# Turning attention probabilities: TensorE and ScalarE's share given to VectorE and to transfers

## What is computed

```python
x = x + tanh(g_ffn[0]) * ffn(layernorm(x))
# ffn, per sample: T = 512 positions, 8 heads of 64, 5 experts of which each head takes 2
q, k = heads(x @ Wq), heads(x @ Wk)
v = einsum('bthe,btek->bhtk', top2(x @ Ws) * sigmoid(x @ Ws), x @ Wv)
probs = softmax(q * 64 ** -0.5 @ k.T)      # 512 x 512 for each head
attn = probs @ v
out = einsum('bthe,bthk,ekd->btd', top2_mask(x @ Wd), attn, Wo)
```

## Time and profile before

| | before |
|---|---|
| times of three executions | 1172.51, 1174.29, 1174.52 us |
| median | 1174.29 us |
| the profiled execution's own time | 1175.16 us |
| its span | 1173.4 us |
| TensorE busy | 1128.9 us, 96% |
| VectorE busy | 915.4 us, 78% |
| ScalarE busy | 634.2 us, 54% |
| GpSimd busy | 657.0 us, 56% |
| share of TensorE in the chain that ended last | 71% |
| transfers | 108.44 MB, 30.7% of the 16 DMA engines' time |

### The profile page before, as it was taken

How to read it: one execution, slowest core, us unless ns; L and a number is a source line. 1 busy time by engine, 2 the same in 40 slices (tenths; PEclk the granted TensorE clock), 3 DMA queues, 4 the chain that set the end, 5 groups by cost and what they waited for, 6 DMA issues and landing times.

```text
span 1173.4 us, 19136 instructions
## 1 busy us (share of the span) xinstructions
PE 1128.9 (96%) x5885; PEld 855.5 (73%) x5885; DVE 915.4 (78%) x1656; ACT 634.2 (54%) x1332; POOL 657.0 (56%) x476
## 2 busy tenths in 40 slices
PE   7999999999999999999999999999999999999998
PEld 6788888888888888876767667667666666667655
DVE  7988887878787857476786886887887886976986
ACT  7634343434343433457566556556556565666654
POOL 2635242424242425439389298397497496595693
PEclk9999999999999999999999999999999999999999
DMA  5341414141414123422323324224233233231140
GB/s 199 143 135 45 135 46 133 46 132 47 132 49 130 57 86 115 148 89 72 90 55 109 88 54 138 59 63 151 54 89 107 54 110 104 52 122 48 47 126 37
DMA packets 76606, 108.44 MB, mean 92 GB/s; under 512 B 7712, under 2 KB 40224, under 8 KB 76576
## 3 DMA queue, kind: packets, MB, share of 16 engines
q1 hardware_dynamic: 76576, 108.07, 30.7%
HBM read 58.76 MB, written 16.78 MB: 64 GB/s over the span
## 4 chain that ended last, share of the span: by engine, by line
PE 71%; DVE 11%; ACT 7%; issue 7%; POOL 3%; DMA 1%; DVEq 0%; ACTq 0%
PE ps_f L992 22%; PE ps_o L2267 9%; PE ps_s L992 7%; PE ps_h L992 6%; PE ps_r L2193 6%; PE ps_r L2226 4%; PE ps_s L2244 4%; ACT probs_odd L1663 4%; PE ps_r L2202 3%; DVE nmax L1853 3%; PE ps_s L2252 3%; DVE z_tmp L1872 2%; ACT tmp L1663 1%; POOL spare L1580 1%; DVE z L1883 1%
## 5 line engine op out<-in xcount | busy, mean ns | idle before, releaser
L1853 DVE TENSOR_REDUCE nmax<-ps_s 128x1 f32<-128x512 f32 x256 | 158.4, 679 | 75.0 <-PE ps_s L2244 74.0
L1580 POOL TENSOR_TENSOR spare<-xv,pick 128x512 f32<-128x512 f32 x160 | 170.6, 1066 | 35.8 <-DVE pick L1968 22.9
L1598 POOL TENSOR_TENSOR z<-z,z_tmp 128x1280 f32<-128x1280 f32 x35 | 102.8, 2937 | 156.0 <-DVE z_tmp L1872 153.7
L1586 POOL TENSOR_TENSOR spare<-spare 128x512 f32<-128x512 f32 x128 | 180.5, 1410 | 10.0
L1663 ACT ACTIVATE probs_odd<-ps_s,nmax 128x512 f32<-128x512 f32 x124 | 146.7, 1183 | 0.0
L1663 ACT ACTIVATE tmp<-ps_s,nmax 128x512 f32<-128x512 f32 x124 | 85.6, 690 | 102.6 <-DVE nmax L1853 102.6
L2267 PE MATMUL ps_o<-pt,spare 128*64 128x512 f32 x496 | 115.0, 606 | 2.3 <-issue 2.3
L254 POOL TENSOR_TENSOR e_t<-e_t 128x512 fp32r<-128x512 f32 x28 | 35.4, 1302 | 135.8 <-ACT e_t L510 135.8
L2244 PE MATMUL ps_s<-k,q 64*128 64x512 f32 x768 | 106.5, 408 | 0.9 <-ACT pt L1672 0.9
L2244 PEld LDWEIGHTS ps_s<-k,q 64*128 64x128 f32 x768 | 67.4, 184 | 46.9 <-issue 34.3
L2252 PE MATMUL ps_s<-ident,probs_odd 128*128 128x128 f32 x512 | 77.4, 279 | 19.6 <-ACT probs_odd L1663 17.9
(11 more groups left out here) (245 smaller groups left out, 2302.0 us busy)
## 6 DMA issues: line engine op xcount, KB each, us to landing
pt<-tmp SPq DMA_DIRECT2D x248, 128.0 KB, 2.6
stage<-in_x SPq DMA_DIRECT2D x32, 256.0 KB, 3.1
x_sb<-in_x SPq DMA_DIRECT2D x8, 1024.0 KB, 5.3
x_dram<-x_sb SPq DMA_DIRECT2D x32, 256.0 KB, 3.2
stage<-x_dram SPq DMA_DIRECT2D x8, 1024.0 KB, 5.5
x_sb<-x_dram SPq DMA_DIRECT2D x8, 1024.0 KB, 5.5
out_dram<-x_sb SPq DMA_DIRECT2D x31, 256.0 KB, 2.6
stage<-in_ctx_t SPq DMA_DIRECT2D x28, 256.0 KB, 2.8
```

The lines of the kernel that those rows point to most:

```text
L1580: pool.tensor_tensor(v_tmp[:] if e else acc, xv[:, :, e, :].unsqueeze(2).broadcast_to(shape), pick[:, e, :, 2 * p:2 * p + 2].unsqueeze(3). ...
L1586: pool.tensor_tensor(acc, acc, v_tmp[:], ALU.add).then_inc(v_steps, 1)
L1598: pool.tensor_tensor(zv, zv, z_tmp[:, h % 2], ALU.add).then_inc(z_pool, 1)
L1853: dve.tensor_reduce(nmax[:, n:n + 1], ps_s[:, n % BANKS, :], AX_X, ALU.max, negate=True).then_inc(nmax_ready, 1)
```

## The change

All four steps of a round go the way of the even ones. Both halves of a round's buffer hold two heads, so `tmp` has room for one round only, and a second buffer, `late`, is laid behind `spare`, which for that is allocated as a part of a larger tile. The order of a buffer's columns gets the head as a further factor, so that a block row's run is 2 KB long, and each of the four transfers of a round carries 256 KB; `pt` has the two heads of a pair interleaved likewise. VectorE turns four tiles in TURNS, TensorE none; `probs_copy`, `probs_odd` and the waits for them are gone, and TensorE writes a bank of `ps_s` again when its exponential is done. ScalarE waits once a round for the move of the round before the last. In the last two rounds of the last sample TensorE turns as before; there ScalarE writes the exponentials in the order of the output and reads the scores with a stride.

```diff
-        probs_even = both.tmp[:].rearrange("p r (j s a) -> p (r j s a)", s=2, a=BLOCK).rearrange(
-            "p (r j s a) -> p r j s a", r=2, s=2, a=BLOCK)
-        probs_odd = sb("probs_odd", [P, BANKS // 2, T])
+        probs = both.tmp[:].rearrange("p k t -> p (k t)"), both.late
...
-        def even_probs(n):
-            return probs_even[:, n // BANKS % 2, :, n % BANKS // 2, :]
+        def blocks(n):
+
+            return probs[n // BANKS % 2].rearrange("p (j i s a) -> p j i s a", i=2, s=2, a=BLOCK)[:, :, n % 2,
+                                                                                              n % BANKS // 2, :]
...
+        def by_rows(p):
+
+            return pt[:, p % 2 * 2:p % 2 * 2 + 2].rearrange("p i k t -> p (i k t)").rearrange(
+                "p (r q k i s a) -> p r q k i s a", r=2, q=QUADS, k=NT, i=2, s=2)
...
             def move_blocks(b, r, first=False):
 
                 p = r // 2
-                sp.wait_ge(blocks_turned, b * ODD_STEPS + (r + 1) * ODD_ROUND)
+                sp.wait_ge(blocks_turned, b * STEPS + (r + 1) * BANKS)
...
                 for q in range(QUADS):
-                    sp.dma_start(by_rows(2 * p % 4)[:, r % 2, q].rearrange("p k s a -> p (k s a)"),
-                                 probs_even[q * BLOCK:(q + 1) * BLOCK, r % 2].rearrange(
-                                     "p (j k) s a -> p j (k s a)", j=QUADS)).then_inc(moved[r % 2], 16)
+                    sp.dma_start(by_rows(p)[:, r % 2, q].rearrange("p k i s a -> p (k i s a)"),
+                                 probs[r % 2][q * BLOCK:(q + 1) * BLOCK].rearrange(
+                                     "p (j u) -> p j u", j=QUADS)).then_inc(moved[r % 2], 16)
...
             def scores_exp(b, n, first):
                 act.wait_ge(nmax_ready, b * STEPS + n + 1)
                 h, t = head_tile(n)
-                scores = ps_s[:, n % BANKS, :]
-                if n % 2 == 0:
-                    if n >= 2 * BANKS or not first:
-
-                        act.wait_ge(moved[n // BANKS % 2], (b * PAIRS + n // PAIR) * MOVED)
-                    out, scores = even_probs(n), scores.rearrange("p (j a) -> p j a", a=BLOCK)
-                else:
-                    if n >= BANKS or not first:
-
-                        act.wait_ge(pt_ps, odd_turned(b, n - BANKS))
-                    out, scores = by_keys(probs_odd[:, n % BANKS // 2, :]), by_scores(scores)
...
+                if n % BANKS == 0 and (n >= 2 * BANKS or not first):
+
+                    act.wait_ge(moved[n // BANKS % 2], (b * PAIRS + n // PAIR) * MOVED)
+                act.activation(blocks(n), ps_s[:, n % BANKS, :].rearrange("p (j a) -> p j a", a=BLOCK), ACT.Exp,
+                               bias=nmax[:, n:n + 1], accum_out=den[:, h, t:t + 1]).then_inc(p_exp, 1)
...
-                act.activation(by_keys(plain_probs(n)), by_scores(ps_s[:, n % BANKS, :]), ACT.Exp, bias=nmax[:, n:n + 1],
+                act.activation(plainly(plain_probs(n)), scores_by_keys(ps_s[:, n % BANKS, :]), ACT.Exp, bias=nmax[:, n:n + 1],
...
-                    if 0 <= n < ROUNDS:
-                        for tile in range(n * BANKS + 1, n * BANKS + BANKS, 2):
-                            probs_copy(b, tile, first)
...
-                dve.transpose(even_probs(n), even_probs(n)).then_inc(blocks_turned, 1)
+                dve.transpose(blocks(n), blocks(n)).then_inc(blocks_turned, 1)
...
-                        for tile in range(n * BANKS, n * BANKS + BANKS, 2):
+                        for tile in range(n * BANKS, n * BANKS + BANKS):
                             turn_blocks(b, tile)
...
-                    pe.wait_ge(pt_ready, odd_turned(b, n + 1 - BANKS))
+                    pe.wait_ge(p_exp, b * STEPS + n + 2 - BANKS)
...
-                pe.wait_ge(pt_ready, odd_turned(b, PAIR * p + PAIR - 1))
                 for r in range(2):
                     pe.wait_ge(moved[r], (b * PAIRS + p + 1) * MOVED)
...
-                        rows = by_rows(p % 2 * 2 + a)[:, :, :, k].rearrange("p r q s a -> p q r (s a)")
+                        rows = by_rows(p)[:, :, :, k, a].rearrange("p r q s a -> p q r (s a)")
...
-                    elif place == TURNS:
-                        for tile in range(n * BANKS + 1, n * BANKS + BANKS, 2):
-                            turn_probs(b, tile)
...
+        spare_late = sb("spare_late", [P, 5 * ND * D // 2])
+        spare = spare_late[:, 0:2 * ND * D].rearrange("p (i k n) -> p i k n", i=2, k=ND)
```

More of the change, by code:

```diff
@@ L87 @@
     spare: object
+    late: object
     tmp: object
@@ L1417, in zt @@
             return half * LAST + k
-        def even_probs(n):
-            return probs_even[:, n // BANKS % 2, :, n % BANKS // 2, :]
+        def blocks(n):
+            return probs[n // BANKS % 2].rearrange("p (j i s a) -> p j i s a", i=2, s=2, a=BLOCK)[:, :, n % 2,
+                                                                                              n % BANKS // 2, :]
         def plain_probs(n):
-            if n % 2:
-                return probs_odd[:, n % BANKS // 2, :]
-            return both.tmp[:, n // BANKS % 2 * 2 + n % BANKS // 2, :]
+            return probs[n // BANKS % 2][:, n % BANKS * T:n % BANKS * T + T]
         def by_keys(columns):
@@ L1433, in by_scores, with plainly, scores_by_keys @@
             return columns.rearrange("p (q k a) -> p q k a", q=QUADS, a=BLOCK)
+        def plainly(columns):
+            return columns.rearrange("p (k a q) -> p k a q", q=QUADS, a=BLOCK)
+        def scores_by_keys(columns):
+            return columns.rearrange("p (q k a) -> p k a q", q=QUADS, a=BLOCK)
         def turned(n):
             h, t = head_tile(n)
[L1437 to L1442, removed]
+            return by_rows(h // 2)[:, t // 2, :, :, h % 2, t % 2].rearrange("p q k a -> p k q a")
+        def by_rows(p):
+            return pt[:, p % 2 * 2:p % 2 * 2 + 2].rearrange("p i k t -> p (i k t)").rearrange(
+                "p (r q k i s a) -> p r q k i s a", r=2, q=QUADS, k=NT, i=2, s=2)
         def scored(n):
@@ L1473, in expert_attention @@
         V_STEPS = 2 * E - 1
-        ODD_STEPS, ODD_ROUND = STEPS // 2, BANKS // 2
         MOVED = QUADS * 16
-        LAST_TURNED = (B - 1) * ODD_STEPS + (CUT + 1) * ODD_ROUND - (CUT + 1) * BANKS
-        def odd_turned(b, n):
-            return b * ODD_STEPS + n // 2 + 1
         def all_turned(n):
-            return LAST_TURNED + n + 1
+            return n + 1 - (CUT + 1) * BANKS
         POOL_SUMS, LAST_PAIR = H - 3, PAIRS - 1
@@ L1676, in last_exp @@
                 h, t = head_tile(n)
[L1677 removed]
+                if n % BANKS == 0:
                     act.wait_ge(moved[n // BANKS % 2], (b * PAIRS + n // PAIR) * MOVED)
[L1679 to L1683 removed]
+                act.activation(plainly(plain_probs(n)), scores_by_keys(ps_s[:, n % BANKS, :]), ACT.Exp, bias=nmax[:, n:n + 1],
                                accum_out=den[:, h, t:t + 1]).then_inc(p_exp, 1)
@@ L2292, in values_half @@
                     for a in range(2):
-                        rows = by_rows(p % 2 * 2 + a)[:, half, :, k].rearrange("p q s a -> p q (s a)")
+                        rows = by_rows(p)[:, half, :, k, a].rearrange("p q s a -> p q (s a)")
                         end = pe.matmul(out[head_rows(a)], v_acc[:, p, k, a, :], rows, start=k == 0, stop=k == NT - 1)
@@ L2400, in program @@
         sb("fill", [P, 8])
+        spare_late = sb("spare_late", [P, 5 * ND * D // 2])
+        spare = spare_late[:, 0:2 * ND * D].rearrange("p (i k n) -> p i k n", i=2, k=ND)
         both = Both(
             x1_norm=x1_norm, x1_stats=x1_stats, ident=sb("ident", [P, P]),
-            x_sb=sb("x_sb", [P, NT, D]), stage=sb("stage", [P, NT, D]), spare=sb("spare", [P, 2, ND, D]),
-            tmp=sb("tmp", [P, ND, T]), c_t2=sb("c_t2", [P, 2, ND, T], F32R), c_2=sb("c_2", [P, 2, NT, D], F32R),
+            x_sb=sb("x_sb", [P, NT, D]), stage=sb("stage", [P, NT, D]),
+            spare=spare, late=spare_late[:, 3 * ND * D // 2:], tmp=sb("tmp", [P, ND, T]), c_t2=sb("c_t2", [P, 2, ND, T], F32R), c_2=sb("c_2", [P, 2, NT, D], F32R),
             es_t2=sb("es_t2", [P, 2, ND, T], F32R), feat_ps=sem("feat_ps"), hc_ready=sem("hc_ready"),
```

5 lines of the change are left out of this document (removed).

## The result

| | before | after |
|---|---|---|
| median of four runs each, same comparison | 1173.40 us | 1181.28 us |
| range | 1172.25 to 1174.52 | 1177.9 to 1182.68 |
| profiled execution, its span | 1175.16, 1173.4 | 1177.9, 1176.1 |
| TensorE, VectorE, ScalarE, GpSimd busy | 1128.9, 915.4, 634.2, 657.0 | 1084.3, 976.6, 529.8, 656.6 |
| mean granted clock | 1.00 | 0.975 |

The ratio is 1.0063 [1.0037, 1.0089]: slower by 0.63%. The profiled execution after is the fastest of its four, 3.4 us under their median, and the one before lies 1.8 above its own, so the two profiles are only 2.7 us apart in span where the medians are 7.9. What the slower three did can't be read from them.

What follows compares the result with a forecast made beforehand. TensorE was taken to set the pass, with VectorE nearly full in D to G. Terms -6.2 (passes), -1.3 (first rounds), +0.3 (end) and +10.5 (clock) summed to +3.3 us: 1177.6 us, range 1164 to 1188.

Steps and rivals of the forecast that it cites:

- the likeliest case: Whole kernel: pass gains are outweighed by a halved TensorE clock after idling; 1173 to 1184 us, chance 0.47.
- the signs of being wrong: In the profile: a short idle stretch on TensorE, a clock staying at 1.0, or ScalarE waiting for moved rounds.
- The rival without a clock loss: Whole kernel: the same schedule with no clock loss, faster at 1167 us, from 1163 to 1171; chance 0.27.
- D to G: Four of the pass's rounds A to H (n = 5 to 12): VectorE becomes the bound; +0.8, +1.22 and -0.6 us.
- the rival in which TensorE goes on setting the pace: Loop passes: VectorE's extra turns mostly fall into waits; 5.8 us less a pass, 1133 us, chance 0.08.
- the slow one: VectorE's turns: one costs more at the new stride or beside doubled transfers; 1185 to 1200 us, chance 0.13.
- A, B, C, H: Pass rounds among n = 5 to 12: relief of 0, -0.64, -0.9 and -0.79 us.
- The idle stretch: Round G: TensorE runs ahead and stands idle some 5.7 us until VectorE's sum, before the turns of z.
- The clock's price: Each pass, after G's idle stretch: a halved clock slows turns of z, values and scores; 1.5 us, seven times +10.5.
- The first rounds: First sample through A's start: shorter exponentials against four turns before the next maxima; -1.3 us, between 0 and twice that.
- The cover named for the transfers: Exponentials of round r + 2 wait for round r's move; a round of 9 us or more covers landings of about 3.
- The end: Second-last values product waits for the last moved round: turns +1.22, landing +0.4, exponentials -1.35; together +0.3 us.

Runs made afterwards that it cites:

- the version with fills: The changed kernel plus 36 dummy transposes of the identity on TensorE in its idle stretch ahead of the turns of z in round G: 1167.60 us.
- the experiment that moves first: The changed kernel with the last sample's moves of round A issued on SyncE ahead of the wait for the stores and the residuals' load: 1178.73 us.
- the kernel with fills at the end alone: The changed kernel plus 76 dummy transposes on TensorE in the idle stretch ahead of the second-last values product, nothing else: 1179.21 us.
- The version with F turned later: The changed kernel with VectorE turning round F's four tiles in G, behind its second sum of z and ahead of G's own: 1160.79 us.
- with fills in G: The kernel turning F later, plus 20 dummy transposes before the turns of z, 60 at the end, and the last sample's first moves issued earlier: 1155.57 us.
- with early turns at the end: The kernel with F turned later and fills in G and at the end, plus VectorE turning the last sample's round A tiles before the products: 1156.59 us.

## Why the prediction was right

The time is slower, 1181.28 in a range of 1164 to 1188 and 3.7 us above the 1177.6, by the mechanism of the likeliest case. As a difference it is more than twice as large, +7.9 us between the medians for +3.3. Of what was to show it, most came: no turns in TensorE's loop, VectorE's turns 248 at the old price, no idle time on VectorE ahead of G's sum, exponentials at 0.69 us, an idle stretch over 4 us and a halved clock in G of each pass. TensorE's busy time and the pass came otherwise: 44.6 us less for about 70, and 0.2 us longer (84.04 for 83.86) for 0.6. And of the signs of being wrong one came once: ScalarE waited for a moved round in the first A. The rival without a clock loss was put at 1167; the experiment that takes just that loss away gave 1167.6. By parts its profile is -4.2 us up to the first A, +2.1 in the first pass, -10.0 in the other six and +4.8 at the end, together -7.3 for the -7.2 summed, so this hit too has errors that cancel. That rival's order of work was right and only its clock wrong, so the sign hung on the clock alone. That VectorE paces D to G is what defeated the rival in which TensorE goes on setting the pace, and a turn of 0.67 us defeated the slow one.

**TensorE's busy time** fell by 44.6 us, not by about 70. The turns were 77.4 before, but they overlap the products beside them: without their instructions the trace of before is busy for 1069.2 us, 59.7 less. The rest is the halved clock, at which the same products count for longer: the version with fills, without its 28.7 us of fills, is at 1069.7.

**A, B, C, H.** Predicted 0, -0.64, -0.9, -0.79 (with D to G -0.91 a pass, which is -6.4 in seven and not -6.2); measured -0.05, -0.73, -0.90, -0.90. In a pass the relief of the slots is what the code's order gives, and no more.

**D to G without the clock.** Predicted 0.8 + 1.22 - 0.6 = +1.42. In the version with fills D to G take 40.35 us in the same pass (736.77 to 777.12), 1.16 more than the 39.19 of the earlier trace rows. A pass there comes to 82.19 on average over six, against 83.86 before: -1.7 for the predicted -0.9. The difference is 0.3 in D to G, 0.3 in A (11.14 us there) and 0.1 each in B and H.

**The idle stretch** was 5.04 us for the predicted 5.7.

**The clock's price** was 1.85 us a pass for 1.5. The single drop at the end of the kernel before was a fair row for the values: 5.35 us there, 4.98 here, for 3.65. The step that took 1.5 "since the turns of z wait 0.7 for VectorE anyhow" gave too much for that: none of the turns starts before the sum is done, and at the halved clock the twelve then took 2.82 us, for the 1.47 that they take before.

**The first rounds.** Predicted -1.3 through A's start, between 0 and twice that; measured -4.6, outside these bounds. 1.4 of it is there at the first scores (502.07 before, 500.70 after), ahead of any turned round, and what it comes from isn't shown; the rest is a larger gain of the alternating rounds than I gave them. But A gives part of it back. The cover named for the transfers fails here, once: the round ahead lasts 7.4 us (527.76 to 535.15) and not 9, and ScalarE waits for a moved round.

```profile
540.33 0.69 ACT L1654 ACTIVATE spare_late<-ps_s,nmax 128x512 f32<-128x512 f32 x1 [3.40 <-DMA pt<-spare_late]
```

The first of A's maxima is ready at 538.38, so 1.9 of the 3.40 us are the move's. This A takes 13.6 us, before 11.75 (539.74 to 551.49), and a halved clock is part of it (the products for k take 4.17 us instead of 3.0). With 2.5 more in D to G the first pass is 2.2 us longer than before. In the passes behind it no exponential waits for a move. In the profile of the experiment that moves first, B starts at 550.93 and not at 548.74, and there the halved clock falls on the values of A (5.35 us) and not on k: this place varies by 2.2 us between runs, and is one part of their spread.

**The end** is the mis-sized term: +0.3 predicted, +4.0 measured. The step said "landing 2.6 us for 128 KB; the nearest row at 256 KB is 3.1". That row is of loads of x, each of which holds SP for 0.34 us; four moves of the new size hold it for 3.9 to 4.1 and land after 4.5 each in the passes, and after 6.1 here. And the step followed the data alone. It left out SP's own queue: H's moves end there at 1129.31, the sample's stores are issued until 1133.36, a load of residuals waits for them to land, and the moves on the path, turned by 1135.97, stand behind all of these until 1136.83. The order of the queue could be read from SP's timeline of before, where it costs nothing, since the tiles there are turned only at 1136.3:

```profile
1136.36 2.64 SPq L1512 DMA_DIRECT2D pt<-tmp  x4
```

By these rows the +4.0 are: the turns +0.8 (for 1.22), the queue's order +0.9 (for nothing), from the first issue to the values 8.53 us against 4.77, +3.8 (for 0.4), and what follows the start of the values -1.5 (for -1.35). The upper end, "up to +2 if four together take long", was still too low.

**The sum** on the profiled execution: first rounds -4.6, first pass +2.2, six passes +1.1, end +4.0, together +2.7. Predicted were +3.0 before the end and +0.3 for it. So the hit is partly two errors that cancel: before the end the time was 4.3 us better than summed, and at the end 3.7 worse. Between the medians, 5.2 us more were lost than between the profiles. Of these, 1.8 are the profile before, which lies that much above its median. The other 3.4 are the change's profile, which lies that much below its median. The experiment that moves first has a profiled run that is its median, and it reaches the last A 1.8 us later than the change's profile does, all of it by the end of the first pass; the 1.6 us that are left weren't found. A second place differs between runs too: of the last six passes of the kernel with fills at the end alone four take 84.4 to 85.0 us, where the change's profile has three such, and the six take 1.1 us more.

## What to carry to other kernels

Before work is moved off the bounding engine, list round by round which engine ends last, since relief counts only in the rounds where the receiving engine has idle time ahead of its next result; here its place in the receiver's queue was worth 20.5 us with the clock that hung on it, more than the whole change. Where the relief leaves the matmul engine idle for some microseconds ahead of work on the path, look for a halved clock behind it and keep the engine at dummy transposes up to just before the awaited result, with a count that ends inside the wait. And where a transfer gets twice as large, read the issuing queue's timeline at the place where a product waits for it, not only the landing time of a lone transfer.

## What the hardware did that was not expected

- Transposes of a 128x128 identity, 36 of them in 4.09 us, held the granted clock at 1.00 through a wait in which it fell to 0.50 in every pass of the change without them. They are worth 13.7 us, 1.2% of the time.
- A wait of 2.65 us ahead of F's scores is followed by a clock of 0.50 in some passes and 1.00 in others. In the version with fills this still happens in three passes (behind 920.5, 1002.4 and 1084.4), and these take 82.1 to 82.3 us like the others, since VectorE is the bound there. In this kernel the halved clock cost time only where TensorE was on the path.
- The version with F turned later has two pass lengths that alternate, 80.0 and 83.9 us, with the same instructions in each; with fills in G they are 81.1 and 82.7, and with early turns at the end only one of the last six passes is long.
- Issuing a move of 256 KB held SP 0.97 us (four in 3.88), and one of 128 KB before 0.63 (four in 2.50, from 705.35); the landing took 4.5 us against 2.6, and 6.1 beside a load of 1 MB.
